# One exponential over both pairs of heads, in place of one for each pair

## The reference, cut to what matters

```python
logits = jnp.einsum('bihd,bjhd->bhij', q, k) * scale + pos_bias[None]
attn = jax.nn.softmax(logits, axis=-1)
out = jnp.einsum('bhij,bjhd->bihd', attn, v).reshape(B, S, D)
return jnp.einsum('bsd,ed->bse', out, Wout)
```

## Time and profile before

| | |
|---|---|
| median of 3 runs | 1992.14 us (1989.74 to 1992.73) |
| the profiled execution | 1986.88 us, its span 1984.8 us |
| mean granted TensorE clock | 0.954 of full speed |
| busy share of the span | PE 87%, DVE 58%, ACT 54%, POOL 49% |
| all exponentials of layer 1 (L1001) | 256, together 273.7 us busy |

### The profile page before, as it was taken

The page is one execution under the profiler, slowest core; times in us unless marked ns, Lnnn a source line. Parts: engine busy times, 40 slices in busy tenths (PEclk is TensorE's granted clock), DMA queues, the critical chain, the costliest instruction groups (busy, mean ns, idle before and its releaser), DMA issues. The chain is left out here.

```text
span 1984.8 us, 32309 instructions
## 1 busy us (share of the span) xinstructions
PE 1733.1 (87%) x11015; PEld 1135.6 (57%) x11015; DVE 1151.9 (58%) x2519; ACT 1064.0 (54%) x1471; POOL 978.1 (49%) x736
## 2 busy tenths in 40 slices
PE   4989888887999999999996967788888788868999
PEld 3455554544788888888885753333334334336566
DVE  5665666662243433534434428988888898826345
ACT  1555555555632323323222325988889899965542
POOL 1444444432434434434342434887887787855102
PEclk7999999998999999999998987999999999978999
DMA  3333333323521201201101172323223232108356
GB/s 115 97 107 90 89 95 94 95 75 122 172 91 40 69 24 58 79 27 58 52 33 51 42 256 76 86 75 90 92 65 107 66 82 80 33 13 314 108 160 207
DMA packets 119261, 182.85 MB, mean 92 GB/s; under 512 B 14197, under 2 KB 73077, under 8 KB 119162
## 3 DMA queue, kind: packets, MB, share of 16 engines
q1 hardware_dynamic: 114300, 175.31, 29.0%
q10 hardware_dynamic: 4224, 4.19, 0.6%
q0 software_dynamic: 640, 2.10, 0.3%
HBM read 90.72 MB, written 39.91 MB: 66 GB/s over the span
## 5 line engine op out<-in xcount | busy, mean ns | idle before, releaser
L839 POOL TENSOR_TENSOR l_prob<-l_prob,l_bias 128x1024 f32<-128x1024 f32 x192 | 452.9, 2379 | 100.9 <-ACT l_prob L998 100.1
L1278 POOL TENSOR_TENSOR f_hl<-f_full,f_hh 128x512 fp32r<-128x512 f32 x192 | 248.1, 1292 | 411.4 <-DVE f_hh L1316 271.0
L1054 DVE CUSTOM_DVE_ANT_0 l_slot<-l_slot,l_bias 128x512 f32<-128x512 f32 x512 | 339.6, 713 | 23.4 <-PE l_slot L1138 23.3
L1001 ACT ACTIVATE l_prob<-l_prob 128x1024 f32<-128x1024 f32 x256 | 273.7, 1076 | 0.5 <-POOL l_prob L839 0.5
L493 DVE TENSOR_REDUCE l_peak<-l_slot 128x2 f32<-128x256 f32 (+3 forms) x256 | 206.2, 821 | 107.1 <-PE l_slot L585 104.7
L1366 PE MATMUL f_ps<-f_hh,f_hi_h 128*128 128x512 f32 x1024 | 260.3, 390 | 3.6 <-ACT f_hh L1290 2.6
L1366 PE MATMUL f_ps<-f_hl,f_hi_h 128*128 128x512 f32 x1024 | 258.3, 389 | 0.0
L397 ACT ACTIVATE l_prob<-l_slot 128x1024 f32<-128x1024 f32 (+3 forms) x256 | 175.3, 706 | 96.9 <-PE l_slot L604 93.8
L1366 PEld LDWEIGHTS f_ps<-f_hh,f_hi_h 128*128 128x128 f32 x1024 | 192.0, 188 | 47.0 <-issue 3.3
L1366 PEld LDWEIGHTS f_ps<-f_hl,f_hi_h 128*128 128x128 f32 x1024 | 192.2, 188 | 39.8
L1298 ACT ACTIVATE f_full<-f_ps,f_h_s 128x512 f32<-128x512 f32 x128 | 86.8, 684 | 235.3 <-PE f_ps L1366 217.0
(11 more groups left out here) (228 smaller groups left out, 2817.0 us busy)
## 6 DMA issues: line engine op xcount, KB each, us to landing
l_stacks<-l_parts SPq DMA_DIRECT2D x384, 128.0 KB, 2.6
f_raw<-in_L_ffn_h_w SPq DMA_DIRECT2D x16, 512.0 KB, 4.2
f_raw<-in_L_ffn_h_w SPq DMA_DIRECT2D x32, 256.0 KB, 2.6
e_w<-in_L_ffn_f SPq DMA_DIRECT2D x32, 256.0 KB, 2.9
l_bias<-ext SPq DMA_DIRECT2D x16, 448.0 KB, 8.0
l_x_in<-in_L_attn_x SPq DMA_DIRECT2D x8, 512.0 KB, 3.9
xh<-l_xh SPq DMA_DIRECT2D x8, 512.0 KB, 2.6
xl<-l_xl SPq DMA_DIRECT2D x8, 512.0 KB, 2.6
```

The costliest lines, as they stand in the source:

```text
L839: return eng.tensor_tensor(probs(n), src, bias[:, h:h + 2, j * P:j * P + T], ALU.add)
L1001: act.activation(probs(n), probs(n), ACT.Exp).then_inc(p_exp.sem, 1)
L1054: ins = dve.tensor_tensor_reduce(src, src, bias[:, 4 * g + 2 * pr + a, t * P:t * P + T], 1.0, 3 * NEG, ALU.add, ALU.max, peak[:, g, a, pr, ...
L1278: pool.tensor_tensor(t.hl[layer % 2][:, o], t.full[:, n % 2], t.hh[layer % 2][:, o].bitcast(F32), ALU.subtract).then_inc(self.h_lo.sem, 1)
```

## The change

ACT's exponential is issued once for each key tile, over its 2048 columns (both pairs), at the place where the second of the two stood. So the events are at even steps only, behind c0 and behind c2; `p_exp` counts 16 in a batch and not 32, and `value` waits for one count for each key tile. The new exponential waits for both bias additions. ACT's order in a cycle is now c0 E, c2 E, c3, with E the exponential of 2048 columns.

```diff
-    b_ps, p_exp = sem("b_ps", STEPS), sem("p_exp", STEPS)
+    b_ps, p_exp = sem("b_ps", STEPS), sem("p_exp", STEPS // 2)
...
         at = s - LAG - TAKEN
-        STEADY.append(("prob_exp", 0 if at >= 0 else -1, at % STEPS))
+        if at % 2:
+            STEADY.append(("prob_exp", 0 if at >= 0 else -1, at % STEPS // 2))
         STEADY.append(("score", 0, s))
...
                 if kind == "prob_exp":
-                    wait(act, *added(n), b)
-                    act.activation(probs(n), probs(n), ACT.Exp).then_inc(p_exp.sem, 1)
+                    for m in (2 * n, 2 * n + 1):
+                        wait(act, *added(m), b)
+                    act.activation(prob[:, n % RING], prob[:, n % RING], ACT.Exp).then_inc(p_exp.sem, 1)
...
-                    wait(pe, p_exp, 2 * n + 2, b)
+                    wait(pe, p_exp, n + 1, b)
```

## The result

The changed kernel takes 2006.74 us (median of 4 runs, 2001.66 to 2010.67) against 1991.0 before (4 runs on the same chip, 1989.74 to 1992.73): ratio 1.0076, 95% interval 1.0057 to 1.0095. It is slower, by 15 us by the ratio (15.7 between the medians), where 8 were forecast. The profiled execution took 2001.66 us, 14.8 more than the one of before; its span is 1999.6.

A forecast was written before the change was run, and what follows sets the result against it. Taken as bound by one chain passing between PE and ACT or DVE, no engine full. Delays 8.4, last round −0.6, end +0.4 sum to +8 us: 2000 us against the 1992.14 median, range 1987 to 2008.

The forecast's parts named there:

- The mechanism: On ACT, the copy c3 and the turned input's rounding queue behind the long exponential and come late; sum +8 us.
- The saving of 12.8 us is hidden: ACT saves 0.10 us on each of 128 pairs, but already idles waiting for PE; 0 gained in the steady part.
- (b): Cycle turning the next input: rounding `xh` starts 0.75 us late behind the exponential; all on the path, 7 times.
- (c): Cycle with the second `mix_turn`: c3 0.85 us late, 0.49 taken up between products; 0.17 left, 6 times.
- (a): Layer norm's last tile between exponential and c3: c3 0.77 us late, partly hidden by the transposition; 0.3 on path, 7 times.
- The end: Last round and layer end: −0.6 us in the last round, then +0.4 at the end.
- −0.6 in the last round: Last round, without `ln` and `qk`: DVE's wait for `mix_turn`'s rounding behind an exponential goes; about 0.6 us back.
- +0.4 behind it: Layer end: POOL's wait for c2 goes, −0.45 us; the longer last exponential, alone on the path, adds 0.87.
- they pass whole: Rival: none of the three cycles' delays is taken up and nothing returns in the last round; 15.7 us, 2008; chance 0.13.
- ACT sets the pace: Rival: ACT's order of work is the limit, so the 12.8 us saving comes through; 1980 us; chance 0.10.
- swallowed: Rival: PE and DVE catch up after the late copies, rounds keep 71.6 us, only +0.4 remains; 1992.5 us; chance 0.22.

The follow-up runs named there:

- The order alone: Changed kernel with each 2048-column exponential issued as two of 1024 back to back at the same place; ratio to the kernel before 1.0076.
- 18 split: Changed kernel with only step 18's large exponential split into two small ones in their old steps; 1993.88 us, ratio to the kernel before 1.0012.
- 18 alone large: Kernel before with one large exponential in a batch, at step 18, the other 15 pairs small in their old places; 1998.63 us, ratio 1.0030.
- 18 and 26 split: Changed kernel with the large exponentials of steps 18 and 26 split into small ones, 14 of 16 left large; 1990.24 us, ratio to the kernel before 1.0005.

## Why the prediction was right, and where it was mis-sized

- **The mechanism.** Right: c3 and small work standing behind a long exponential. The order alone gives 1.0076, the size alone nothing that can be seen.
- **The saving of 12.8 us is hidden.** Right. ACT's copies wait 17.7 us more for PE, and two small exponentials in place of each large one (1.0076) are no slower than the large ones (1.0068 and 1.0076). E holds ACT for 1.81 us (1369.12 to 1370.93), where 1.82 was taken.
- **(b), 0.75 us.** Right to the hundredth, by the cycle: 10.53 before, 11.28 after, 10.53 with 18 split, 11.28 with 18 alone large. In the first batch the cycle goes from 9.91 to 10.72, 0.81 more, with S0 behind c3.
- **(c), 0.17 us.** Right in sum: the two cycles took 8.52 + 8.53, and now 8.42 + 8.80. I had not seen that the first of them would gain 0.10 and the second lose 0.27.
- **(a), 0.3 us.** Right in size by luck. At full clock the two cycles took 8.88 + 8.67 = 17.55, and now 8.40 + 9.44 = 17.84: 0.29 more. But c3's lateness is not half hidden by the transposition: S0 waits 1.18 and not 0.42, and the cycle grows by all of it, 0.77 us. What takes 0.48 back is a term that the prediction put at nothing: GpSimd, which gets c0 and c2 earlier, adds earlier, so that DVE's shift ends earlier and PE's 1.87 us become 1.39.
- **The first batch.** Left out: where there is no `mix_turn` yet, the cycle of step 26 goes from 7.28 to 8.14 us, since S0 waits 1.63 us for c3 where it was 0.78. That is 0.86 once.
- **The end, −0.2 us.** Two parts. Of the −0.6 in the last round: right. From P1's addition of the last batch to the last addition it was 52.11 us at full clock, and 51.44 in the changed kernel run again, also at full clock: −0.67. The +0.4 behind it stays open: from the last addition to the end of the last exponential it was 10.66 us before, and 10.53 and 11.26 in the two profiles of the changed kernel. The last exponential did cost the 0.87 (1.91 us and not 1.06).
- **What was left out, and makes the size.** The clock. The prediction took the round at 71.6 with its one fall, and added delays at full speed. Up to the last addition of the stage the delays at full clock come to 0.81 + 6 x 0.76 for (b), 6 x 0.29 for (a), 6 x 0.18 for (c), 0.86 in the first batch and −0.67 in the last: 8.4 us, where the prediction had 7.8. Measured are 12.4 (86.26 to 89.18 us from the first addition to 1297.50 and 1304.70, 358.14 to 365.84 in the five rounds, 101.81 to 103.64 behind them). The other 4 us are the falls: 0.7 to 0.8 us in each of five rounds before, and after 0, 2.7, 0, 2.8 and 0, and some 2.6 more in the first and the last batch. The remaining 2.3 of the profile's 14.8 is from other stages: 4.3 ahead of the first addition of layer 1, where the two kernels are the same, −1.9 behind the last.

So the place and the path were right and the schedule's part of the size too, the latter with two errors that cancel in (a). The measured 2006.74 us lie near the upper end of the stated range, and what brought them there, the clock, is no term of the sum. In the working, two small figures are off: by the slope the lower bound for E comes to 1.70 us and not 1.73, and the chances for slower add up to 0.63 and not 0.64.

The rival "they pass whole" came nearer with 2008 us, but for another reason than its own: (b) and (c) passed as forecast, (a) passed whole but gave 0.48 of its 0.77 us back in front of itself, and the clock made up the rest. "ACT sets the pace" is refuted by the slower time itself and by the two small ones at the new place, which hold ACT longer and take the same time; "swallowed" is refuted by the cycles.

By the Trainium skill ("Perfetto Trace Analysis", Optimizing Scalar/DVE Operations) breaking instructions up may help where ACT isn't saturated but holds others up. The trace agrees: split at step 18 alone, the kernel goes from 1.0068 to 1.0012.

No version measured beats the kernel before. For the schedules with an expected 70.5 us at full clock the gain to be had was 0.3 us a round, and no round of theirs ran at full clock; in the profile of the one with 18 and 26 split the falls cost more (up to 1.5 us each, where it was 0.7 to 0.8). Why is not shown.

## What to carry to other kernels

Before two instructions of an in-order engine are merged, ask what used to run between them, and which consumer of the work behind them is next in a hurry; the fixed cost saved (0.1 us here) is small against one such wait (0.75). A delay cured by moving the instruction may turn up at the next consumer, so check the cycle's length and not the wait. And where the clock of TensorE falls in every round, take the round's length at full clock and with a fall as two numbers, in both kernels: 70.55 us against 71.6 looked like a gain of 1.05, against 70.87 it was 0.3. And work that comes earlier may matter on a side that nobody waits for directly, as GpSimd's did here (0.48 us).

## What the runs showed of the hardware

VectorE's shift on 4 columns took 2.13 us in six of its seven executions in the kernel before (0.15 in the other), and it ended together with GpSimd's addition that had begun just before it:

```profile
1414.03 2.36 POOL L839 TENSOR_TENSOR l_prob<-l_prob,l_bias 128x1024 f32<-128x1024 f32 x1 [0.45 <-ACT l_prob L998]
...
1414.28 2.13 DVE L1034 SCALAR_TENSOR_TENSOR l_shift<-l_moments,l_rstd 128x4 f32<-128x4 f32 x1
```

1414.03 + 2.36 = 1416.39 and 1414.28 + 2.13 = 1416.41. By the Trainium skill ("SBUF — State Buffer", SBUF: two separate sides) a VectorE operation with two SBUF inputs and a GpSimd one share a pair of ports that one of them holds for a whole instruction; the trace agrees. Taking it off VectorE changed nothing in the time, 0.9999.

What a fall of the clock costs depends on where it lands. A single one lasts about 3.4 us, and it cost 0.7 to 0.8 us in the kernel before, 0.3 with step 18 split, and 0.1 to 1.5 with 18 and 26 split.

The spread of one kernel goes with the clock in part: the four runs of the changed kernel with a granted clock of 0.949, 0.945, 0.945 and 0.946 took 2001.7, 2010.7, 2007.4 and 2006.1 us. The last three differ by 4.6 us at nearly one clock.
